# The context's three products in one contraction of 128 rows, in the last stage of a recommender kernel

## What is computed

```python
h = jnp.concatenate([z, dense_ctx], axis=1)        # 2048 x (256 + 16)
h = jnp.maximum(h @ W_top1 + b_top1, 0.0)          # 272 -> 512
h = jnp.maximum(h @ W_top2 + b_top2, 0.0)          # 512 -> 256
y = h @ W_top3                                     # 256 -> 1
```

## Time and profile before

| | |
|---|---|
| median of three runs | 2424.73 us (2424.66 to 2425.77) |
| the profiled execution | 2426.18 us |
| its span | 2424.2 us, so 2.0 us lie around it |
| mean granted TensorE clock | 0.994 of full speed |
| TensorE busy | 2343.5 us, 97% of the span |
| VectorE busy | 2253.4 us, 93% |
| GpSimd busy | 2004.7 us, 83% |
| ScalarE busy | 1306.0 us, 54% |

### The profile page before, as it was taken

One profiled execution on the slowest core, in us unless ns is written; L12 is line 12 of the kernel. 1 busy time (PEld: TensorE's weight loads), 2 busy tenths in 40 slices (PEclk: granted clock), 3 DMA queues, 4 the chain that ended last, 5 costly groups with the idle time before them and its releaser, 6 DMA issues.

```text
span 2424.2 us, 32379 instructions
## 1 busy us (share of the span) xinstructions
PE 2343.5 (97%) x7936; PEld 1497.1 (62%) x7936; DVE 2253.4 (93%) x2241; ACT 1306.0 (54%) x1534; POOL 2004.7 (83%) x1284
## 2 busy tenths in 40 slices
PE   1699999999999999999999999999999999999999
PEld 0466666666666666666666666666666666666655
DVE  2699999999999999999999999999999999999973
ACT  2355555555555555555555555555555555555542
POOL 3689888988888898888889888888988888898630
PEclk9899999999999999999999999999999999999999
DMA  7878778877877887787788778778877877887710
GB/s 180 175 197 231 188 200 219 216 183 210 233 191 196 219 212 185 212 234 187 200 219 214 184 211 232 187 200 221 208 190 209 233 182 205 221 209 188 204 56 1
DMA packets 403715, 475.43 MB, mean 196 GB/s; under 512 B 171409, under 2 KB 180625, under 8 KB 403425
## 3 DMA queue, kind: packets, MB, share of 16 engines
q1 hardware_dynamic: 304354, 310.69, 52.9%
q10 hardware_dynamic: 78864, 159.39, 21.5%
q0 software_dynamic: 20480, 5.15, 1.8%
HBM read 465.41 MB, written 9.71 MB: 196 GB/s over the span
## 4 chain that ended last, share of the span: by engine, by line
PE 94%; POOL 2%; DMA 2%; issue 1%; SPq 0%; ACT 0%; DVE 0%; ACTq 0%; POOLq 0%
PE z L709 91%; POOL rows L507 1%; DMA xb<-x_rows 1%; POOL low L537 1%; DMA x_rows<-rows 1%; DMA rows<-table,index 0%; SPq L411 0%; PE x L804 0%; PE z L823 0%; PE prod_dve L804 0%; PE z L825 0%; PE z L782 0%; PE z L828 0%; PE x L805 0%; PE x L806 0%
## 5 line engine op out<-in xcount | busy, mean ns | idle before, releaser
L537 POOL TENSOR_TENSOR low<-prod_pool,high 128x1024 fp32r<-128x1024 f32 (+1 forms) x576 | 1379.9, 2396 | 220.8 <-ACT high L877 214.1
L709 PE MATMUL z<-prod_whole,w_whole 128*128 128x512 f32 (+2 forms) x2432 | 1129.4, 593 | 41.7 <-DVE prod_whole L592 41.7
L709 PE MATMUL z<-high,w_high 128*128 128x512 f32 (+1 forms) x1792 | 863.9, 482 | 31.2 <-ACT high L877 16.2
L877 ACT ACTIVATE high<-prod_pool 128x1024 fp32r<-128x1024 f32 (+1 forms) x576 | 610.9, 1061 | 405.8 <-DVE prod_pool L592 236.3
L709 PEld LDWEIGHTS z<-prod_whole,w_whole 128*128 128x128 f32 (+2 forms) x2432 | 460.9, 190 | 426.1 <-issue 364.1
L507 POOL DMA_INDIRECT rows<-table,index x640 | 613.5, 959 | 115.2 <-issue 99.7
L709 PE MATMUL z<-high,w_low 128*128 128x512 f32 (+1 forms) x1792 | 708.3, 395 | 0.0
L592 DVE TENSOR_TENSOR prod_pool<-xh,x 128x1024 f32<-128x1024 f32 x512 | 622.6, 1216 | 38.8 <-ACT x L855 33.6
L592 DVE TENSOR_TENSOR prod_whole<-xh,x 128x1024 f32<-128x1024 f32 (+1 forms) x576 | 615.7, 1096 | 7.6 <-PE z L709 1.6
L877 ACT ACTIVATE high<-prod_dve 128x1024 fp32r<-128x1024 f32 (+2 forms) x384 | 339.0, 883 | 497.0 <-DVE prod_dve L592 323.4
L709 PE MATMUL z<-low,w_high 128*128 128x512 f32 (+1 forms) x1664 | 553.5, 426 | 4.2 <-POOL low L537 4.2
(11 more groups left out here) (59 smaller groups left out, 404.6 us busy)
## 6 DMA issues: line engine op xcount, KB each, us to landing
xh<-x_rows SPq DMA_DIRECT2D x63, 2560.0 KB, 17.8
xh<-x_rows ACTq DMA_DIRECT2D x63, 2432.0 KB, 19.2
xb<-x_rows SPq DMA_DIRECT2D x128, 546.0 KB
xb<-x_rows SPq DMA_DIRECT2D x64, 468.0 KB
xa<-x_rows SPq DMA_DIRECT2D x192, 78.0 KB
rows<-table,index POOLq DMA_INDIRECT x640, 5.4
xh<-x_rows SPq DMA_DIRECT2D x65, 128.0 KB, 20.5
x_rows<-rows SPq DMA_DIRECT2D x256, 20.0 KB, 1.6
```

Source lines behind the costliest of these rows:

```text
L537: pool.tensor_tensor(low[0:g.rows, g.split_slot, 0:n, :], prod_pool[0:g.rows, g.slot, 0:n, :], high[0:g.rows, g.split_slot, 0:n, :].bitcas ...
L709: return pe.matmul(z[stage][:, :], weights[0:g.rows, table[stage, g.tiles[i]], :], src[0:g.rows, i, :], start=g.begins_layer and first, st ...
L877: act.activation(high[0:g.rows, g.split_slot, 0:n, :], src[0:g.rows, 0:n, :], ACT.Copy).then_inc(high_ready, 1)
```

## The change

The host now gives `ctx_t` and `wt1c` as arrays of 128 rows: the 16 rows stand at rows 0, 32 and 64, and all other rows are zero. Both are loaded whole, and ScalarE rounds all 128 rows. VectorE then makes low parts in place: of the weights in rows 32 to 47, of the context in rows 64 to 79. One contraction over 128 rows so adds hi(w)hi(x) (rows 0 to 15), lo(w)hi(x) (rows 32 to 47) and hi(w)lo(x) (rows 64 to 79). The separate low tiles of the context are no longer used. In layer one the three passes of 16 rows are replaced by one of 128 rows.

```diff
+CTX_LOW_WEIGHTS, CTX_LOWS = 32, 64
+CTX_ROWS = 128
...
-        wt1c_sb = flat[0:CTX, 2048:2048 + T1]
-        ctx_sb = flat[0:CTX, 2560:2560 + B]
+        wt1c_sb = flat[0:CTX_ROWS, 2048:2048 + T1]
+        ctx_sb = flat[0:CTX_ROWS, 2560:2560 + B]
...
-                    "wt1c": w[0:CTX, 2 * T1:3 * T1],
+                    "wt1c": w[0:CTX_ROWS, 2 * T1:3 * T1],
...
-                    "ctx": [w[0:CTX, CTX_AT:CTX_AT + MB], w[0:CTX, CTX_AT + MB:CTX_AT + 2 * MB]],
+                    "ctx": [w[0:CTX_ROWS, CTX_AT + m * MB:CTX_AT + (m + 1) * MB] for m in range(2)],
...
             def mlp_low_part(i):
                 name, src = mlp_weights[i]
                 dve.wait_ge(mlp_high, i + 1)
-                dve.tensor_tensor(lo[name], src, hi[name].bitcast(f32),
-                                  ALU.subtract).then_inc(mlp_low, 1)
+                rounded, into = hi[name], lo[name]
+                if name == "wt1c":
+                    rows = slice(CTX_LOW_WEIGHTS, CTX_LOW_WEIGHTS + CTX)
+                    src, rounded = src[rows], rounded[rows]
+                    into = rounded
+                dve.tensor_tensor(into, src, rounded.bitcast(f32), ALU.subtract).then_inc(mlp_low, 1)
...
-                    dve.tensor_tensor(lo[name][m % 2], src, hi[name][m % 2].bitcast(f32),
-                                      ALU.subtract).then_inc(inputs_low, 1)
+                    rounded, into = hi[name][m % 2], lo[name][m % 2]
+                    if name == "ctx":
+                        src, rounded = src[CTX_LOWS:CTX_LOWS + CTX], rounded[CTX_LOWS:CTX_LOWS + CTX]
+                        into = rounded
+                    dve.tensor_tensor(into, src, rounded.bitcast(f32), ALU.subtract).then_inc(inputs_low, 1)
...
-                    ks.append(((hi["wt1c"][:, js], lo["wt1c"][:, js]),
-                               (hi["ctx"][m % 2], lo["ctx"][m % 2])))
                     for i, ((wh, wl), (xhi, xlo)) in enumerate(ks):
                         pe.matmul(z_h1[j], wh, xhi, start=i == 0, stop=False)
                         pe.matmul(z_h1[j], wl, xhi, start=False, stop=False)
-                        mm = pe.matmul(z_h1[j], wh, xlo, start=False, stop=i == 2)
+                        pe.matmul(z_h1[j], wh, xlo, start=False, stop=False)
+                    mm = pe.matmul(z_h1[j], hi["wt1c"][:, js], hi["ctx"][m % 2], start=False, stop=True)
                     mm.then_inc(hidden1_done, 1)
...
+    def stacked(rows):
+        out = np.zeros((CTX_ROWS, rows.shape[1]), rows.dtype)
+        for at in (0, CTX_LOW_WEIGHTS, CTX_LOWS):
+            out[at:at + CTX] = rows
+        return out
...
-        "ctx_t": np.ascontiguousarray(a["dense_ctx"].T),
+        "ctx_t": stacked(a["dense_ctx"].T),
...
-        "wt1c": np.ascontiguousarray(wt1[4 * H:]),
+        "wt1c": stacked(wt1[4 * H:]),
```

## The result

| | before | after |
|---|---|---|
| median | 2424.66 us (5 runs, 2423.95 to 2425.77) | 2412.05 us (5 runs, 2410.46 to 2412.64) |
| profiled execution | 2426.18 us | 2412.64 us |
| its span | 2424.2 us | 2410.0 us |

The ratio is 0.9947, 95% interval 0.9933 to 0.9962: 12.6 us less. The forecast was 12.9 us as the likeliest (2411.8 us), with bounds of 11.4 to 13.5 (2413.3 to 2411.2 us).

A forecast was written before the change was run, and what follows sets the result against it. TensorE was taken as the bound, with 94% of the chain and the MLP its alone. 12.72 us over four steps plus 0.19 at layer two made 12.9 off the 2424.73 median: 2411.8 us, range 2409.8 to 2417.5.

The forecast's parts named there:

- Passes and turns: MLP layer one: 28 passes of 128 rows and no turn, 3.18 us less a step; 12.9 us with layer two's entry.
- The third layer's entry: Third layer in steps 1 to 3, now behind 128 rows: gain from nothing to 0.56 us; none taken.
- Rounding and low parts: ScalarE rounding 128 rows: nothing to 0.07 us more; VectorE's in-place low parts: nothing to 0.02 each; no loss taken.
- Loads: SP's queue carries 1120 KB more; context lands at about 2318 to 2321, before ScalarE's wait at 2331.5; nothing lost.
- Engines that follow: VectorE and ScalarE keep up with blocks every 1.64 us; tightest is step 0's fourth cast, with 1.3 us of cover.
- Passes only: Rival, layer one: operand change makes the turns, so they stay and only passes go, 7.5 us, 2417.3; 8%.
- The exposed weight load: Rival, layer one: 128-row weight loads wait for the running pass, 8.3 us more, 2433.0; 1%.
- The late load: Rival, ScalarE's wait at L918: context lands after 2331.5, each us late costs one; some loss (2414.3) 3%, slower 1%.
- A main loop whose end moves by more than 1 us: Sign of error in the new profile; a shift of several us in the loop was given 6%.

The follow-up runs named there:

- the second timing: The changed kernel, unaltered, timed again in the same rounds as the version with three further edits: 2412.75 us, ratio 0.9945.
- the wide weights: The changed kernel with the third layer's weights widened by zeros to 128 columns, in a tile and load of their own: 2411.36 us.
- The late load: The changed kernel with the context's load issued about 20 us later, after ScalarE's relu of stage 1 of chunk 63: 2419.14 us.
- the first experiment: The kernel before, with the context's operands zero-padded to 128 rows, still nine passes a block: 2419.25 us, ratio 0.9977.
- three edits: The changed kernel with 128-column third-layer weights, `wt1` and `wt1c` rounded later, and four filling products in TensorE's wait: timed 2408.68 us, ratio 0.9932.
- later rounding: The changed kernel with ScalarE rounding `wt1` and `wt1c` behind the first two roundings of stage 2 of chunk 63: 2409.71 us.

## Why the prediction was right

*Passes and turns.* Right in mechanism and within 0.3 us in size. The sum was 12.9 us, the MLP gave 13.19. The term that was off is the pass: taken as 0.2336 us from layer two, it measures 6.47 / 28 = 0.231 in layer one, so a step took 6.47 us and not 6.54, 0.28 us in four steps. A turn is by that more than the 0.187 taken: 5.67 / 29 = 0.196. The two shares, expected as 7.5 for passes and 5.4 for turns, were measured apart as 7.43 and 5.67. That the medians, too, lie within 0.3 us of the forecast is in part luck: they also carry the start and the hand-over, which moved by 1.91 and 0.77 us between the two profiles, and the second timing's ratio of 0.9945 stands for some 13.3 us.

*The third layer's entry.* No row of before showed it behind 128 rows, with bounds of nothing to 0.56 us; nothing was taken. It still takes 1.81 us behind 128 rows, so nothing was the right end, and the wide weights show that its own shape is why. The price was smaller than the 0.19 that the upper bound took, though: the entry costs 0.09 us.

*Rounding and low parts.* ScalarE's 128x512 rounding and VectorE's low part in place, from the timeline of the kernel after:

```profile
2345.95 0.62 ACT L957 ACTIVATE w_high<-xh 128x512 fp32r<-128x512 f32 x1
...
2347.33 0.68 DVE L689 TENSOR_TENSOR w_high<-xh,w_high 16x512 fp32r<-16x512 f32 x1
```

They are 0.62 and 0.68 us, as with 16 rows. TensorE's wait at the hand-over is 4.63 us, as before.

*Loads.* The DMA issues of the kernel after:

```profile
xh<-ctx_t SPq DMA_DIRECT2D x1, 1024.0 KB, 7.4
```

Issued at 2308.76, it landed at 2316.2, 13.5 us ahead of ScalarE's rounding at 2329.74. The forecast of 2318 to 2321 went from an issue at 2310.54, so it was 7.5 to 10.5 us from issue to landing; the 7.4 lie at its lower end. The late load shows the price that the cover saved.

*Engines that follow.* In step 0 VectorE's fourth cast ends at 2358.31 and layer two, begun at 2356.70, needs it 12 passes later, at 2359.5: 1.2 us of cover, 1.3 forecast.

*The rivals.* Passes only (2417.3) fell with the first experiment. The exposed weight load fell with the 0.23 of L816: loads of 0.19 us run under the pass before them. By the Trainium skill, "TensorE: Matmul & The Clock Gate", Part 3, The mechanism, weight loads overlap with running matmuls only where the row group differs; the trace disagrees, with 128-row loads that follow each other every 0.23 us without idle time. What is exposed here is the load where the number of rows changes from 128 to 64 or less, behind 0.36 us of idle time with 16 rows and 0.37 with 64. The late load was possible and did not happen. A main loop whose end moves by more than 1 us was named as a sign of error; it moved by 1.78 us, but with the first matmul, and the next profile of the same kernel has its relu at 2330.03, later than before's.

## What to carry to other kernels

Small matmuls that add into the same output can stand in one contraction: at 512 columns a pass of 16 rows costs as much as one of 128, 0.23 us, so three passes of 16 rows with their two turns (0.89 us on the chain and 0.20 more behind them, 1.09 a block) became one pass of 0.23. Look at the first pass behind each change of shape before counting passes: here 43% of the gain (5.67 of 13.10 us) was turns, and zero padding alone took it. A load that grows eightfold is free only as far as its cover reaches; read the landing and the wait, not the share of DMA.

## What the runs showed of the hardware

Turns, of 0.19 to 0.20 us, come at weights of 64, 32 and 16 rows beside 128, and not at 80 and 96. Beside 128 columns, weights of one column turn too, with 0.09 in and 0.20 out.

TensorE's wait of 4.6 us at the hand-over let the granted clock fall from 1.00 to 0.50, the lower of its two levels, and where it fell differed between executions of one kernel. Slices of 1 us of the changed kernel, in the wait (TensorE busy 0.00):

```profile
2331.00:2332.00 1.00, 0.00 (x0) 0.00 (x0) 1.00 (x1) 1.00 (x2) 0.00 (x0) 0.50 0.00 0
```

And of the changed kernel again, in the wait and behind it:

```profile
2333.00:2334.00 1.00, 0.00 (x0) 0.00 (x0) 1.00 (x2) 1.00 (x3) 0.00 (x0) 1.00 0.00 0
...
2336.00:2337.00 1.00, 1.00 (x3) 0.48 (x2) 1.00 (x2) 0.56 (x1) 1.00 (x2) 0.50 0.00 0
```

Read in slices of 0.1 us, it fell 2.8 us behind the relu in the first, while TensorE still waited, and was back 9.6 us behind it; in the second it fell at 5.2, with TensorE at work again, and was back at 8.6. The mean over the hand-over is 0.92 in six traces with 21.2 to 21.7 us, and 0.85 in two with 22.1 and 22.4. With passes put into the wait it stayed at 1.00, in three traces with 19.6 to 20.0 us.

Where one kernel was traced twice, the start differs most: the first matmul came at 39.78 and 41.88 us in the changed kernel, and at 41.59 and 39.44 in the one with three edits. Over all traces it lies between 38.95 us (later rounding) and 41.88, while from it to the relu of chunk 63 every trace takes 2287.5 to 2288.6 us.
